# A small language-model layer on one core: gate and up weights under two scales, eight chunks split early, twelve of sixteen units of block 1 by fp16 halves

## The chip, the cores and the metric

The kernel runs on one NeuronCore of a Trainium2 chip. Its time is the device time of one execution in microseconds (us). The trace names the engines PE (TensorE matmuls), PEld (TensorE's loads of stationary operands), DVE (VectorE), ACT (ScalarE), POOL (GpSimd) and SP (SyncE, whose queue starts most DMAs).

## What is computed

The reference, with ids x of shape (2, 1024), vocabulary 128, width 512, 32 query heads and 8 key heads of width 16, hidden width 2048:

```python
h = rms_norm(rms_norm(emb[x]) * norm_w @ proj.T)          # token part
a = layernorm(h)
att = softmax(causal(q(a) @ k(a).T / 4)); h = h + (att @ v(a)) @ wo
g = layernorm(h)
h = h + (silu(g @ w_gate.T) * (g @ w_up.T)) @ w_down.T    # FFN
```

As there are only 128 different tokens, keys and values are tables over the vocabulary, and the weights of the attention are multiplied by counts of how often a token has been seen.

## The kernel before, in words

The 2048 tokens are eight **blocks** of 256, each of two tiles of 128. Block n's attention runs beside the FFN of block n-1, in `phase(n, att, ffn, m)`, which every engine goes through on its own in 24 **slots**; block 0 has no FFN beside it. Nothing is scheduled by a tool: which engine does what in which slot is written out in tables of slots (`FIRST_SLOTS`, `SECOND_SLOTS`, `HI_FIRST`, ...), each engine works through its own list in order, and semaphores hold it where it needs another engine. An engine that waits holds back all that stands behind it in its list.

**A unit of attention** V (16 a block, one a slot in slots 0 to 15) is one key head of one tile with its four query heads: PE transposes the queries into PSUM (`turn`, L1062), `stack` copies them to SBUF (ACT in blocks 0 and 1, L504; DVE later, L809), PE makes scores (`score`, L1073), ACT their exponentials (L529), DVE clips them and multiplies by the counts (L843), PE multiplies by the values (`values`). The last step has two forms. A `wide` unit takes the float32 weights as they are (L1091), two slots after its scores. A unit by **halves** is split into two fp16 parts, high by ACT (L539), low by POOL (L394), and takes eight short fp16 matmuls (L1097, L1098), three slots after its scores. All of block 0 is wide, all from block 2 on is halves; in block 1 `HALF_PAIRS` says which pairs of units are halves. `TAIL_PAIRS` says which pairs use another PSUM bank.

**A chunk of the FFN** j (16 a block) is gate and up for 128 hidden values: 24 matmuls on PE (L1120, L1121, L1125) in slot j, then in slot j+1 ACT's tanh (L521), two DVE steps (L831, L836), ACT's fp16 high half (L533) and POOL's low half (L390). In slots 16 to 23 PE does the down product in eight parts.

**The weights** of the FFN arrive as float32, 24 chunks of 128x1024 in 12 pairs (0 to 15 gate and up, 16 to 23 down). Each chunk is split once into two fp16 halves after a scaling by a power of two: `split_high` on ACT (L497) at the end of a slot, `split_low` on DVE (L786) in the same slot or the next. The scale of gate and up, `s_gu`, comes from a bound: PE forms Gram matrices of all 16 chunks (`gate_up_gram`, L1053, 128 matmuls spread over the start of block 0), DVE takes the diagonal in slot 12 (`gate_up_diag`, L752), PE sums it in slot 13 (L1143), and DVE makes the scale in slot 13 (`weight_scales`, L756 to L760). The first four chunks are split in slots 13 to 23 of block 0 (`HI_FIRST`, `LOW_FIRST`), the other twenty in slots 0 to 19 of block 1 (`HI_NEXT`). Wo is split in slots 1, 2, 5 and 10 of block 0 under its own scale (L487 on ACT, L747 on DVE).

**Ends of blocks.** After the last units of a tile come the transposes of y (L1156), its fp16 halves (ACT L564, DVE L869), the Wo product (L1167 to L1173), the residual (L877), the layer norm, its transposes (L1178) and their halves (L573, L892), in slots from 11 on. In slot 22 DVE's `place_max` (L794 to L801) puts the next block's row maxima in place, and PE's first `turn` of the next block, in slot 23, waits for it:

```python
if att and n > 0 and s == 23 and n + 1 < BLOCKS:
    turn((n + 1) * UPB)          # begins with pe.wait_ge(m_rdy, tl + 1)
```

## Time and profile before

| | |
|---|---|
| median of 3 runs | 717.11 us (717.09 to 717.43) |
| the profiled execution | 717.22 us, its span 715.5 us |
| mean granted TensorE clock | 0.986 of full speed |
| PE busy | 688.6 us (96%) |
| DVE, ACT, POOL busy | 410.2 (57%), 333.4 (47%), 313.4 (44%) |
| block 0's attention and tail | about 47 to 91 us of the span |
| block 1's slots 0 to 15 | 94.2 to 149.4 us |
| DMA | 40.37 MB, most of it before 76 us |

Shares of the whole span are means over stages with different limits; the change lies in the first quarter of the span, so the stretches 44 to 91 us and 94 to 176 us are what is to be read. In rows in order of time the columns are start, duration, engine, line, operation, tiles; "x8" joins eight neighbours, and square brackets give the idle time of the engine just before and who ended it. The next instruction of an engine often starts a little before the shown end of the one before it, so the cost of a row in a queue is the distance from its start to the next start. A row of a stretch gives its length, then the busy us (and instructions) of PE, PEld, DVE, ACT and POOL, then the granted clock, the DMA share and GB/s. A row of the waits gives the us in total, the number of waits and the longest.

### The profile page before, as it was taken

The numbers are of one execution on the slowest core, as the hardware profiler recorded it, in microseconds if no ns is written. First come the engines' busy times: TensorE is split into PE (matmuls) and PEld (weight loads), VectorE is DVE, ScalarE is ACT, GpSimd is POOL, SyncE is SP. The second block draws the span as 40 slices with busy tenths as digits, with TensorE's granted clock in tenths as the row PEclk, the third lists the DMA queues.
The fourth block names the chain that finished last, engine by engine and source line by source line (L and its number), as shares of the span: only waits on it lengthen the run. The fifth ranks groups of instructions, "written<-read, shape, count | busy, mean of one in ns | idle before, by whom it ended". The sixth has DMA issues, their size and how long they took to land.

```text
span 715.5 us, 16315 instructions
## 1 busy us (share of the span) xinstructions
PE 688.6 (96%) x6399; PEld 525.3 (73%) x6399; DVE 410.2 (57%) x1019; ACT 333.4 (47%) x676; POOL 313.4 (44%) x410
## 2 busy tenths in 40 slices
PE   8459999999999999999999999999999999999998
PEld 5359688965997479866996589856996599747873
DVE  7767789886655465545656365445655465543320
ACT  6426377861665146621664156522663166512320
POOL 5020315761565436751675336552665256511220
PEclk9859999999999999999999999999999999999999
DMA  8759500011000110012000300011000200000000
GB/s 316 288 206 404 191 18 1 3 47 61 17 2 2 60 63 1 2 47 77 2 1 2 106 17 2 1 61 62 2 2 16 93 16 2 1 16 16 2 1 29
DMA packets 10459, 40.37 MB, mean 56 GB/s; under 512 B 1808, under 2 KB 2576, under 8 KB 8592
## 3 DMA queue, kind: packets, MB, share of 16 engines
q1 hardware_dynamic: 6912, 25.44, 9.1%
q0 software_dynamic: 3328, 13.11, 5.9%
q8 instruction: 51, 0.84, 0.5%
q10 hardware_dynamic: 144, 0.79, 0.3%
q14 instruction: 24, 0.20, 0.1%
HBM read 29.89 MB, written 9.44 MB: 55 GB/s over the span
## 4 chain that ended last, share of the span: by engine, by line
PE 80%; DVE 10%; ACT 5%; issue 2%; DMA 1%; SPq 0%; ACTq 0%; DVEq 0%
PE banks L1120 13%; PE banks L1125 13%; PE banks L1121 13%; PE banks L1226 6%; PE banks L1228 6%; PE banks L1227 6%; PE banks L1073 3%; PE banks L1091 2%; PE banks L1167 2%; PE banks L1062 2%; PE banks L1173 2%; PE banks L1168 2%; DVE gate_work L831 2%; DVE ffn_weights L786 1%; PE banks L1053 1%
## 5 line engine op out<-in xcount | busy, mean ns | idle before, releaser
L1121 PE MATMUL banks<-xnT_and_h,ffn_weights 128*128 128x256 f16 x1024 | 237.3, 272 | 0.0
L1120 PE MATMUL banks<-xnT_and_h,ffn_weights 128*128 128x256 f16 x1024 | 237.2, 272 | 0.0
L390 POOL TENSOR_TENSOR gated_split<-gate_work,gated_split 128x256 f16<-128x256 f32 x128 | 88.4, 691 | 243.0 <-ACT gated_split L533 243.0
L1125 PE MATMUL banks<-xnT_and_h,ffn_weights 128*128 128x256 f16 x1024 | 153.6, 273 | 0.0
L394 POOL TENSOR_TENSOR weights_split<-weights,weights_split 128x512 f16<-128x512 f32 x104 | 123.2, 1185 | 0.0
L1120 PEld LDWEIGHTS banks<-xnT_and_h,ffn_weights 128*128 128x128 f16 x1024 | 100.4, 98 | 11.4
L1125 PEld LDWEIGHTS banks<-xnT_and_h,ffn_weights 128*128 128x128 f16 x1024 | 100.2, 98 | 11.6
L1121 PEld LDWEIGHTS banks<-xnT_and_h,ffn_weights 128*128 128x128 f16 x1024 | 99.9, 98 | 11.4
L521 ACT ACTIVATE gate_work<-banks,scales 128x256 f32<-128x256 f32 x128 | 60.6, 474 | 99.1 <-PE banks L1125 99.1
L529 ACT ACTIVATE weights<-banks,scales 128x512 f32<-128x512 f32 x128 | 87.3, 682 | 14.0 <-PE banks L1073 14.0
L843 DVE SCALAR_TENSOR_TENSOR weights<-weights,counts_T 128x512 f32<-128x512 f32 x128 | 87.6, 685 | 9.1 <-ACT weights L529 9.0
L809 DVE COPY q_stack<-banks 128x256 f16<-128x256 f16 x96 | 27.8, 290 | 103.0 <-PE banks L1062 103.0
L831 DVE SCALAR_TENSOR_TENSOR gate_work<-gate_work,banks 128x256 f32<-128x256 f32 x128 | 52.9, 413 | 58.7 <-ACT gate_work L521 58.2
L533 ACT ACTIVATE gated_split<-gate_work 128x256 f16<-128x256 f32 x128 | 53.3, 417 | 69.1 <-DVE gate_work L836 69.1
L1228 PE MATMUL banks<-ffn_weights,gated_split 128*128 128x512 f16 x224 | 84.9, 379 | 0.0
L1227 PE MATMUL banks<-ffn_weights,gated_split 128*128 128x512 f16 x224 | 84.9, 379 | 0.0
L1226 PE MATMUL banks<-ffn_weights,gated_split 128*128 128x512 f16 x224 | 84.8, 379 | 0.0
L539 ACT ACTIVATE weights_split<-weights 128x512 f16<-128x512 f32 x104 | 63.8, 613 | 0.0
L836 DVE SCALAR_TENSOR_TENSOR gate_work<-banks,gate_work 128x256 f32<-128x256 f32 x128 | 54.3, 425 | 4.4
L346 POOL DMA_INDIRECT token_rows<-token_table,indices x16 | 15.7, 980 | 89.1 <-DVE xnT_and_h L877 82.9
L573 ACT ACTIVATE xnT_and_h<-banks 128x512 f16<-128x512 f32 x16 | 9.6, 597 | 80.5 <-PE banks L1178 75.0
L1073 PE MATMUL banks<-q_stack,k_stack_even 128*128 128x128 f16 x256 | 42.7, 220 | 1.2 <-ACT q_stack L504 1.2
(236 smaller groups left out, 1043.4 us busy)
## 6 DMA issues: line engine op xcount, KB each, us to landing
ffn_weights<-in_ffn_w SPq DMA_DIRECT2D x12, 1024.0 KB, 9.9
out_rows_dram<-ffn_weights SPq DMA_DIRECT2D x16, 256.0 KB, 2.0
xnT_and_h<-in_wqkv SPq DMA_DIRECT2D x1, 1536.0 KB, 8.7
local_table<-gated_split SPq DMA_DIRECT2D x2, 640.0 KB, 5.3
local_table<-xnT_and_h SPq DMA_DIRECT2D x2, 640.0 KB, 5.8
gated_split<-in_projT SPq DMA_DIRECT2D x4, 256.0 KB, 4.3
ffn_weights<-in_wo SPq DMA_DIRECT2D x1, 1024.0 KB, 10.7
token_table<-weights_split ACTq DMA_DIRECT2D x1, 768.0 KB, 6.0
```

Source lines behind the costliest of these rows:

```text
L390: g.tensor_tensor(gtl[:, j, :], g2[j % 2], gth[:, j, :], ALU.subtract).then_inc(gt_lo, 1)
L394: g.tensor_tensor(WTl[V % RING], E[V % RING][:, :], WTh[V % RING], ALU.subtract).then_inc(wt_lo, 1)
L529: a.activation(E[V % RING][:, :], b_S[V % 2], ACT.Exp, scale=c_exp).then_inc(exp_done, 1)
L831: v.scalar_tensor_tensor(ag[j % 2], th[j % 2], 1.0, f_bank[j % 3][:, 0:BLK], ALU.add, ALU.mult).then_inc(a_rdy, 1)
L843: v.scalar_tensor_tensor(w, w, SEEN_MAX, cT[:, t * P:(t + 1) * P].unsqueeze(1).broadcast_to([P, REP, P]), ALU.min, ALU.mult).then_inc(w_rd ...
L1073: last = t.matmul(b_S[V % 2][:, (2 * j + a) * P:(2 * j + a + 1) * P], (KstA, KstB)[a][:, gr * P:(gr + 1) * P], Qst[:, r * 256 + j * P:r * ...
L1120: t.matmul(o, wh, xTh[m % 2][:, c, :], start=c == 0, stop=False)
L1121: t.matmul(o, wl, xTh[m % 2][:, c, :], start=False, stop=False)
L1125: last = t.matmul(o, gu_w(s, up, c, 0), xTl[m % 2][:, c, :], start=False, stop=c == DC - 1)
L1226: t.matmul(o, hh, dn_w(j, 0), start=j == 0, stop=False)
L1227: t.matmul(o, hh, dn_w(j, 1), start=False, stop=False)
L1228: last = t.matmul(o, hl, dn_w(j, 0), start=False, stop=j == HC - 1)
```

## The change

Gate and up get two scales. The first, for chunks 0 to 7, comes from sums of squares that ACT forms ahead of block 0 (`for i in range(EARLY // 2)`), summed over partitions by the same small matmul as Wo's; the second, for chunks 8 to 15, from Gram matrices of those chunks alone, now in slots 4 to 11. Where PE did the other Gram matmuls it now does narrow matmuls of no use to the output (`narrow_fill`). The eight early chunks are split from slot 3 of block 0 on, so that sixteen are left for block 1, on a new table of slots. Pairs 12 and 14 of block 1 join the halves (units 24, 25, 28 and 29 of the 16 to 31), pairs 11 and 13 leave the tail bank, and from unit 22 on DVE does the `stack` in place of ACT. `c_tanh` and the factor of L836 become columns per half. Line numbers of the changed kernel are 12 to 26 higher.

```diff
-HALF_PAIRS = (9, 11, 13, 15)
-TAIL_PAIRS = (9, 11, 13)
+HALF_PAIRS = (9, 11, 12, 13, 14, 15)
+TAIL_PAIRS = (9,)
+DVE_STACK = UPB + 6
+EARLY = 8
...
-HI_FIRST = {13: 0, 16: 1, 17: 2, 21: 3}
-LOW_FIRST = {13: (0,), 21: (1,), 22: (2,), 23: (3,)}
-HI_NEXT = {i - 4: i for i in range(4, NCH)}
+HI_FIRST = {3: 0, 6: 1, 8: 2, 10: 3, 13: 4, 17: 5, 21: 6, 22: 7}
+LOW_FIRST = {4: (0,), 7: (1,), 9: (2,), 11: (3,), 13: (4,), 21: (5,), 22: (6,), 23: (7,)}
+HI_NEXT = dict(zip((0, 1, 3, 5, 7, 8, 10, 11, 13, 14, 15, 16, 17, 18, 19, 20), range(EARLY, NCH)))
...
-GU_LEAD = (6, 12)
-GU_GRAM = {0: (12, 26), 1: (26, 38), **{s: (20 + 9 * s, 29 + 9 * s) for s in range(2, 12)}}
+LEAD_FILL = 10
+GU_FILL = {0: 16, 1: 14, 2: 10, 3: 9, **{s: 1 for s in range(4, 12)}}
+GU_GRAM = {s: (32 + 8 * s, 40 + 8 * s) for s in range(4, 12)}
...
-        s_q, s_k, s_v, s_wo, s_gu, s_d = (col(8 + i) for i in range(6))
-        r_q, r_k, r_v = (col(16 + i) for i in range(3))
-        c_exp, c_vo, c_tanh, c_gu, c_out, c_a = (col(20 + i) for i in range(6))
+        s_q, s_k, s_v, s_wo, s_d = (col(8 + i) for i in (0, 1, 2, 3, 6))
+        s_gu = [col(12), col(13)]
+        r_q, r_k, r_v, r_ga = (col(16 + i) for i in range(4))
+        c_exp, c_vo, c_gu, c_out, c_a = (col(20 + i) for i in (0, 1, 3, 4, 5))
+        c_tanh, c_pair = [[col(i), col(i + 1)] for i in (26, 28)]
...
-            sp.wait_ge(tab["wo_sq"], 1)
+            sp.wait_ge(tab["wo_sq"], 1 + EARLY // 2)
...
+            for i in range(EARLY // 2):
+                actq.wait_ge(ffn_in[i], 16)
+                if i > 0:
+                    actq.wait_ge(tab["wo_sq"], i)
+                a.activation(t_sq[:, (i + 1) % 2 * 2 * CH:((i + 1) % 2 + 1) * 2 * CH], raw_pair(i), ACT.Square, accum_out=pm[:, 36 + i:37 + i]).then_inc(tab["wo_sq"], 1)
...
-                    actq.wait_ge(tab["gu_scaled"], 1)
+                    actq.wait_ge(tab["scaled"], 1)
+                if i == EARLY:
+                    actq.wait_ge(tab["gu_scaled"], 2)
...
-                a.activation(half(i, 0), raw(i), ACT.Copy, scale=s_gu if i < 16 else s_d).then_inc(split_hi, 1)
+                a.activation(half(i, 0), raw(i), ACT.Copy, scale=s_gu[i // EARLY] if i < 16 else s_d).then_inc(split_hi, 1)
...
-                    if att and n <= 1 and s + 1 < UPB:
+                    if att and s + 1 < UPB and n * UPB + s + 1 < DVE_STACK:
...
-                root_powers(POWWO, f_bank[0][:, 0:1], 1)
-                v.tensor_scalar(s_wo, sc[:, 60:61], 2.0 ** 14, None, ALU.mult)
+                v.tensor_copy(pm[:, 44:45], f_bank[0][:, 0:1])
+                link(v.tensor_reduce(pm[:, 45:46], f_bank[0][:, 1:1 + EARLY // 2], AX.X, ALU.add))
+                root_powers(POWWO, pm[:, 44:46], 2)
+                v.tensor_scalar(sc[:, 11:13], sc[:, 60:62], 2.0 ** 14, None, ALU.mult)
+                v.tensor_scalar(r_ga, sc[:, 61:62], 1.0, None, ALU.mult)
                 v.tensor_scalar(c_vo, pw(POWV), pw(POWWO), 2.0 ** -14 / QKV_UP, ALU.mult, ALU.mult).then_inc(tab["scaled"], 1)
...
-                link(v.tensor_reduce(pm[:, 44:45], b_tail[:, P:2 * P], AX.X, ALU.max))
-                root_powers(POWG, pm[:, 44:45], 1)
-                v.tensor_scalar(s_gu, sc[:, 60:61], 2.0 ** 14, None, ALU.mult)
-                v.tensor_scalar(c_tanh, pw(POWG), 2.0 ** -26, None, ALU.mult)
-                v.tensor_scalar(c_gu, pw(POWG), pw(POWG), None, ALU.mult).then_inc(tab["gu_scaled"], 1)
-                dve.wait_ge(tab["gu_scaled"], 1)
+                link(v.tensor_reduce(pm[:, 46:47], b_tail[:, P:2 * P], AX.X, ALU.max))
+                root_powers(POWG + 1, pm[:, 46:47], 1)
+                v.tensor_scalar(s_gu[1], sc[:, 60:61], 2.0 ** 14, None, ALU.mult).then_inc(tab["gu_scaled"], 1)
+                v.tensor_scalar(sc[:, 26:28], sc[:, POWG:POWG + 2], 2.0 ** -26, None, ALU.mult)
+                v.tensor_tensor(sc[:, 30:31], pw(POWG), pw(POWG + 1), ALU.max)
+                link(v.tensor_tensor(sc[:, 31:32], r_ga, sc[:, 60:61], ALU.min))
+                v.tensor_scalar(c_gu, sc[:, 30:31], sc[:, 30:31], None, ALU.mult)
+                link(v.tensor_scalar(sc[:, 32:34], sc[:, POWG:POWG + 2], sc[:, 31:32], None, ALU.mult))
+                link(v.tensor_tensor(sc[:, 34:36], sc[:, 32:34], sc[:, 32:34], ALU.mult))
+                v.tensor_scalar(sc[:, 28:30], sc[:, 34:36], 2.0 ** -47, None, ALU.mult).then_inc(tab["gu_scaled"], 1)
+                dve.wait_ge(tab["gu_scaled"], 2)
...
-                    if att and n > 1 and s + 1 < UPB:
+                    if att and s + 1 < UPB and n * UPB + s + 1 >= DVE_STACK:
...
-                        v.scalar_tensor_tensor(g2[j % 2], f_bank[j % 3][:, BLK:2 * BLK], 2.0 ** -47, ag[j % 2],
+                        v.scalar_tensor_tensor(g2[j % 2], f_bank[j % 3][:, BLK:2 * BLK], c_pair[j // EARLY], ag[j % 2],
...
-            pe.wait_ge(tab["wo_sq"], 1)
-            t.matmul(f_bank[0][:, 0:1], ones32, pm[:, 35:36], start=True, stop=True).then_inc(tab["wo_sum"], 1)
+            pe.wait_ge(tab["wo_sq"], 1 + EARLY // 2)
+            t.matmul(f_bank[0][:, 0:1 + EARLY // 2], ones32, pm[:, 35:36 + EARLY // 2], start=True, stop=True).then_inc(tab["wo_sum"], 1)
...
-                    last = t.matmul(f_bank[2][:, 0:P], w, w, start=u == 0, stop=u == 127)
+                    last = t.matmul(f_bank[2][:, 0:P], w, w, start=u == 64, stop=u == 127)
                 return last
+
+            def narrow_fill(count):
+                for _ in range(count):
+                    t.matmul(b_tail[:, 0:P], id16[:, :], cT[:, 0:P], start=True, stop=True)
...
+                    if n == 0:
+                        narrow_fill(GU_FILL.get(s, 0))
...
-            gate_up_gram(0, GU_LEAD[0])
+            narrow_fill(LEAD_FILL)
             turn(0)
-            gate_up_gram(*GU_LEAD)
+            narrow_fill(LEAD_FILL)
```

What this does to an engine's list is seen in the order of its instructions. DVE, block 0, slots 8 to 12, before: L843 is the clipping of a unit, L850 and L853 end a pair of units, L747 is Wo's low half, L869 that of y, and the last row is the Gram diagonal.

```order
L843 SCALAR_TENSOR_TENSOR weights1<-weights1,counts_T 128x512
L747 SCALAR_TENSOR_TENSOR wo_split<-ffn_weights,scales,wo_split 128x1024
L843 SCALAR_TENSOR_TENSOR weights2<-weights2,counts_T 128x512
L850 RECIPROCAL rden1<-banks 128x8
L853 TENSOR_TENSOR xnT_and_h1<-banks,rden1 128x128
L869 TENSOR_TENSOR yT_split<-banks,yT_split 128x512
L843 SCALAR_TENSOR_TENSOR weights0<-weights0,counts_T 128x512
L752 TENSOR_TENSOR gate_work<-banks,ident 128x128
```

The same place in the changed kernel (L863, L870 and L873, L762, L889, and L767 for the diagonal):

```order
L870 RECIPROCAL rden0<-banks 128x8
L873 TENSOR_TENSOR y<-banks,rden0 128x128
L806 SCALAR_TENSOR_TENSOR ffn_weights<-ffn_weights,scales 128x1024
L863 SCALAR_TENSOR_TENSOR weights1<-weights1,counts_T 128x512
L762 SCALAR_TENSOR_TENSOR wo_split<-ffn_weights,scales,wo_split 128x1024
L863 SCALAR_TENSOR_TENSOR weights2<-weights2,counts_T 128x512
L870 RECIPROCAL rden1<-banks 128x8
L873 TENSOR_TENSOR xnT_and_h1<-banks,rden1 128x128
L889 TENSOR_TENSOR yT_split<-banks,yT_split 128x512
L806 SCALAR_TENSOR_TENSOR ffn_weights<-ffn_weights,scales 128x1024
L863 SCALAR_TENSOR_TENSOR weights0<-weights0,counts_T 128x512
L767 TENSOR_TENSOR gate_work<-banks,ident 128x128
```

Three of the new rows L806, the low halves of chunks 1 to 3, stand ahead of the diagonal; the one of chunk 0 stands further up, in slot 4.

DVE, end of block 1, slots 21 and 22, before: L888 is the normalised row block, and the three rows of `place_max` follow it.

```order
L888 TENSOR_SCALAR xn<-xnT_and_h1,ln_stats 128x512
L794 TENSOR_TENSOR max_local0<-max_local0,max_group0 128x32
L799 TENSOR_SCALAR token_rows0<-max_local0 128x2x16
L801 SCALAR_TENSOR_TENSOR token_rows0<-max_local0,token_rows0 128x2x16
L892 SCALAR_TENSOR_TENSOR xnT_and_h1<-banks,xnT_and_h1 128x4x128
```

In the changed kernel:

```order
L908 TENSOR_SCALAR xn<-xnT_and_h1,ln_stats 128x512
L806 SCALAR_TENSOR_TENSOR ffn_weights<-ffn_weights,scales 128x1024
L814 TENSOR_TENSOR max_local0<-max_local0,max_group0 128x32
L819 TENSOR_SCALAR token_rows0<-max_local0 128x2x16
L821 SCALAR_TENSOR_TENSOR token_rows0<-max_local0,token_rows0 128x2x16
L912 SCALAR_TENSOR_TENSOR xnT_and_h1<-banks,xnT_and_h1 128x4x128
```

The low half of the last chunk (L806), which stood a slot earlier, now lies between the normalised rows and `place_max`.

PE, from the small sum ahead of block 0 to slot 0, before (L1053 the Gram matmuls, L1062 a `turn`, L1073 scores):

```order
L1044 MATMUL banks<-part_max,xnT_and_h 128x1
L1053 MATMUL banks<-ffn_weights 128x128 x6
L1062 MATMUL banks<-ident,token_rows 128x128 x2
L1053 MATMUL banks<-ffn_weights 128x128 x6
L1073 MATMUL banks<-q_stack,k_stack_even 128x128
L1073 MATMUL banks<-q_stack,k_stack_odd 128x128
L1073 MATMUL banks<-q_stack,k_stack_even 128x128
L1073 MATMUL banks<-q_stack,k_stack_odd 128x128
L1062 MATMUL banks<-ident,token_rows 128x128 x2
L1053 MATMUL banks<-ffn_weights 128x128 x14
```

In the changed kernel (L1078 the narrow fill, L1086 the turn, L1097 scores):

```order
L1064 MATMUL banks<-part_max,xnT_and_h 128x5
L1078 MATMUL banks<-counts_T,ident 128x128 x10
L1086 MATMUL banks<-ident,token_rows 128x128 x2
L1078 MATMUL banks<-counts_T,ident 128x128 x10
L1097 MATMUL banks<-q_stack,k_stack_even 128x128
L1097 MATMUL banks<-q_stack,k_stack_odd 128x128
L1097 MATMUL banks<-q_stack,k_stack_even 128x128
L1097 MATMUL banks<-q_stack,k_stack_odd 128x128
L1086 MATMUL banks<-ident,token_rows 128x128 x2
L1078 MATMUL banks<-counts_T,ident 128x128 x16
```

Twelve Gram matmuls ahead of the first scores have become twenty fills, and fourteen behind them sixteen.

## Rows read from the trace of the kernel before

**Rows 1.** busy time by engine in two stretches, named in each row
```profile
56.00:78.00 22.00, 21.94 (x249) 19.76 (x246) 17.31 (x47) 13.13 (x25) 0.00 (x0) 1.00 0.94 375
...
94.00:152.00 58.00, 56.48 (x582) 50.17 (x583) 51.67 (x84) 48.26 (x96) 30.88 (x31) 1.00 0.01 2
```

**Rows 2.** PE up to slot 0 of block 0, and its clock
```profile
47.53 1.70 PE L1053 MATMUL banks<-ffn_weights 128*128 128x128 bf16 x14
...
50.00:52.00 2.00, 2.00 (x27) 2.00 (x26) 1.50 (x7) 1.80 (x3) 0.00 (x0) 0.88 0.80 319
```

**Rows 3.** ACT in order of time, slots 0 and 1 of block 0
```profile
46.48 0.38 ACT L504 ACTIVATE q_stack<-banks 128x256 f16<-128x256 f16 x1 [16.79 <-PE banks L1062]
...
51.07 1.15 ACT L487 ACTIVATE wo_split<-ffn_weights,scales 128x1024 f16<-128x1024 f32 x1 [0.20 <-DVE scales L742]
```

**Rows 4.** DVE in order of time, slots 4 to 13 of block 0
```profile
56.56 0.69 DVE L843 SCALAR_TENSOR_TENSOR weights<-weights,counts_T 128x512 f32<-128x512 f32 x1
...
59.24 1.28 DVE L747 SCALAR_TENSOR_TENSOR wo_split<-ffn_weights,scales,wo_split 128x1024 f16<-128x1024 f32 x1
60.43 1.41 DVE L843 SCALAR_TENSOR_TENSOR weights<-weights,counts_T 128x512 f32<-128x512 f32 x2
...
70.81 0.28 DVE L752 TENSOR_TENSOR gate_work<-banks,ident 128x128 f32<-128x128 f32 x1
...
75.40 1.28 DVE L786 SCALAR_TENSOR_TENSOR ffn_weights<-ffn_weights,scales 128x1024 f16<-128x1024 f32 x1 [1.35 <-ACT ffn_weights L497]
```

**Rows 5.** DVE: what it waited for between 56.5 and 70.85
```profile
DVE weights L843 <- ACT weights L529: 2.6, 4, 1.0
```

**Rows 6.** PE in order of time, slots 13 and 16 of block 0
```profile
71.14 0.49 PE L1143 MATMUL banks<-gate_work,xnT_and_h 128*128 128x128 f32 x2
...
77.43 0.81 PE L1091 MATMUL banks<-v_full_one,weights 128*128 128x17 f32 x6
```

**Rows 7.** PE in block 1: first matmul of slots 5 to 10 and 15
```profile
108.76 0.22 PE L1073 MATMUL banks<-q_stack,k_stack_even 128*128 128x128 f16 x1
...
112.34 0.23 PE L1073 MATMUL banks<-q_stack,k_stack_even 128*128 128x128 f16 x1 [0.26 <-ACT q_stack L504]
...
117.08 0.22 PE L1073 MATMUL banks<-q_stack,k_stack_even 128*128 128x128 f16 x1
...
120.90 0.22 PE L1073 MATMUL banks<-q_stack,k_stack_even 128*128 128x128 f16 x1
...
123.85 0.22 PE L1073 MATMUL banks<-q_stack,k_stack_even 128*128 128x128 f16 x1
...
127.01 0.22 PE L1073 MATMUL banks<-q_stack,k_stack_even 128*128 128x128 f16 x1
...
145.04 0.22 PE L1073 MATMUL banks<-q_stack,k_stack_even 128*128 128x128 f16 x1
```

**Rows 8.** ACT in order of time, slots 8 and 15 of block 1
```profile
122.29 0.47 ACT L521 ACTIVATE gate_work<-banks,scales 128x256 f32<-128x256 f32 x1
...
123.71 0.42 ACT L533 ACTIVATE gated_split<-gate_work 128x256 f16<-128x256 f32 x1 [0.37 <-DVE gate_work L836]
...
124.55 1.13 ACT L497 ACTIVATE ffn_weights<-ffn_weights,scales 128x1024 f16<-128x1024 f32 x1
...
148.08 0.59 ACT L564 ACTIVATE yT_split<-banks 128x512 f16<-128x512 f32 x1
```

**Rows 9.** PE, slot 16 of block 1: the first Wo matmul
```profile
149.44 0.39 PE L1167 MATMUL banks<-wo_split,yT_split 128*128 128x512 f16 x1
```

**Rows 10.** one line of the kernel on POOL: duration ns min/median/max
```profile
L394 POOL TENSOR_TENSOR weights_split<-weights,weights_split x104: 1151/1157/2144, 105.7 to 626.7; 128x512 f16<-128x512 f32 x104
```

**Rows 11.** DVE, slot 22 of block 1, and PE in slot 23
```profile
173.17 0.18 DVE L794 TENSOR_TENSOR max_local<-max_local,max_group 128x32 f32<-128x32 f32 x1
...
173.67 0.30 DVE L801 SCALAR_TENSOR_TENSOR token_rows<-max_local,token_rows 128x32 f16<-128x32 f32 x1
...
174.49 0.28 PE L1062 MATMUL banks<-ident,token_rows 128*128 128x128 f16 x2
```

4 lines of the change are left out of this document (2 added, 2 removed).

## The prediction

> **What bounds the kernel now.** I read the stretches first, then each engine in order of time. In block 0's attention PE is full, but DVE has work for 17.3 of 22.0 us [rows 1]; its gaps up to the Gram diagonal are four waits for ACT, 2.6 us together [rows 5]. In block 1 PE has 56.5 of 58.0 us, with DVE at 51.7 and ACT at 48.3 [rows 1], so three engines are near their limit and PE is the one that is full. A slot of block 1 is read from one first score matmul to the next [rows 7]: slot 8, in which no `values` stand, takes 123.85 - 120.90 = 2.95; slot 9, with one unit by halves, 127.01 - 123.85 = 3.16; slot 7, with one wide unit, 120.90 - 117.08 = 3.82. A wide unit thus costs PE 0.87, one by halves 0.21. From block 2 on nothing is changed but the source of one factor (L836), on an engine with slack there. The account is of the stretches 45 to 91 and 94 to 176 us.
>
> **Squares ahead of block 0: 0.** ACT forms four sums of squares of 128x2048. Its copy with scale of half that width takes 1.13 [rows 8], so I take 2.2 each, 8.8 together. ACT is idle 16.8 us ahead of its first `stack` [rows 3]; that hides them. Were that cover gone, PE's small sum would come up to 8.8 later.
>
> **Fills for Gram matmuls: +0.7.** Fourteen Gram matmuls occupy 1.70 from first start to last end, a pitch of 0.107 [rows 2]; the fills have the same 128 columns, so the same pitch. Eight more ahead of the first scores are 0.86, two more in slot 0 0.2, two more in slot 1 under 0.2. The clock is at the lower of its two levels (0.50, 1.2 GHz) and a mean of 0.88 over 50 to 52 puts its rise to 2.4 GHz at 50.5 [rows 2]. PE is no less busy before it with fills, so I let it rise at the same time; what is still to do then goes at double speed, which takes back some 0.4. But ACT's Wo half in slot 1 waits for DVE's scale, with 0.20 of idle time [rows 3], and that scale now comes behind a later first unit, with two more short steps. I take 0.7 for all that follows; at best the extra fills lie in slack, 0; at worst none of it is given back, 1.2.
>
> **Four splits into slots 3 to 12 of block 0: +2.0 more.** ACT has room: a split is 1.04 of its list (1.13 less the overlap) [rows 8], and only the first, behind the two Wo halves, makes the next `stack` late, by about 0.15. DVE has not. Before, unit 4 is clipped at 56.56 and the Gram diagonal starts at 70.81: 14.25, of which 2.6 idle, leaves 11.65 of work [rows 4, 5]. A low half of 128x1024 (Wo's is as wide) occupies 59.24 to 60.43, 1.2 [rows 4], and four of them now stand ahead of the diagonal: 4.8. The clip of unit 4 comes about 1.0 later, for the late start (0.7 + 0.15) and the order in which ACT does split and exponential. The list then has no gap: 56.56 + 1.0 + 11.65 + 4.8 = 74.0 for the diagonal, 3.2 later than 70.81. PE's sum of it stands in slot 13 ahead of Wo, the scores of unit 14 and all else, and follows 0.33 behind the diagonal (71.14) [rows 4, 6]; PE would be there by 72.8 and waits. Some comes back: before, DVE stood 1.35 for ACT's high half of chunk 0, which had waited for the scale, and so unit 14 was clipped late and PE's `values` of it began only at 77.43 [rows 4, 6]. Chunk 4 now has its scale long before. The longer scale in slot 13 eats about half of that. I give back 0.5: block 0's attention ends 3.2 - 0.5 = 2.7 later, 0.7 of it from above, 2.0 from here. The tail up to 91 us is one chain and moves as a whole. Bounds: 1.8 together (no late start, DVE then at the diagonal by 73) and 3.4.
>
> **Four wide units by halves in block 1: -2.6.** 4 x (0.87 - 0.21) = 2.64 on a full PE [rows 7].
>
> **Fewer splits and stacks in block 1: -1.1.** Slot 5 takes 3.58 against 3.16, and slot 6 4.74 against 2.95 + 0.87 + 0.21 = 4.03: 0.42 + 0.71 of waits [rows 7], the first on ACT's `stack` as the 0.26 of idle time at 112.34 says. With no split in slots 2, 4 and 6 and unit 22 stacked by DVE, I take both as gone.
>
> **ACT at the end of block 1: +1.0.** From tanh to the FFN's high half ACT needs 122.29 to 123.71, 1.42; that half and a unit's high half take 0.84 more; a split 1.04 [rows 8]. That is 3.3, in every other slot some 0.3 more for a copy of value sums (an estimate), where PE's slot is now 3.16. Slots 10 and 11, 13 and 14 have splits: ACT comes out of slot 12, which has none, some 0.35 behind, slot 13 adds 0.2 and slot 14 0.45, 1.0 in all. Before the Wo product stands a chain: ACT's copy of y started at 148.08, Wo 1.36 later [rows 8, 9]. In slot 15 the copy now starts 1.0 + 1.42 + 0.84 = 3.3 in, Wo at 4.6; PE is there at 3.5 (the 4.40 of before [rows 7, 9], less 0.66 for the unit and 0.25 for the wait already in it). It waits 1.1 instead of 0.25: 0.9, and 0.1 for a PSUM bank that ACT frees late in slot 12. Bounds 0 and 2.5.
>
> **The last low half ahead of `place_max`: +0.7.** The chain on DVE is tied to PE's Wo product, so 1.2 of low half moves `place_max` from 173.17 to 174.4; with its 0.80 (to 173.97) the maxima are ready at 175.2, where PE's `turn`, at 174.49 [rows 11], waits 0.7, and the last part of the down product behind it. Bounds 0.4 and 1.3.
>
> **Sum.** 0.7 + 2.0 - 2.6 - 1.1 + 1.0 + 0.7 = +0.7 on the profiled execution's 717.22 (span 715.5, 1.7 around it) gives 717.9; the median of the runs is 0.11 lower, so 717.8. A difference under 0.2%, 1.4 us, I call none.
>
> **Rivals.** *Faster: DVE's list in block 0 is absorbed.* It decides at the diagonal in slot 12: if DVE is there by 71 to 72, PE's sum never waits. For it: ACT and PE are ahead there and the idle time was DVE's alone. Against it: 4.8 of new work against 2.6 of gaps [rows 5]. With block 0 at +0.5 in place of +2.7 the time is 715.6 less the 0.6 that ACT's smaller backlog in block 1 would then also be worth: 715.0. Chance 0.23.
>
> *Slower: the late slots of block 1 are bound by ACT, DVE and POOL.* POOL's low half of a unit takes 1.15 at least and 2.14 at most [rows 10]. Its other work is at most (30.9 - 8 x 1.15) / 16 = 1.35 a slot [rows 1, 10], so a slot of POOL is 2.5 or 3.5 against PE's 3.16. If the long form holds in eight late slots, that is 0.33 in each, 2.6, of which I take 0.5 to be in the 1.0 already charged: 2.1 more, 719.9. It decides when POOL is more than 2 us behind, since the lag of three slots covers that much. Chance 0.22. The Trainium skill, page SBUF — State Buffer, section Who interferes with whom, has the rule: DVE and GpSimd share one port pair as an exclusive lock, and an instruction with two SBUF inputs on the one fully blocks a reading one on the other. By that rule each of the four added POOL steps may cost its 1.0 in full, 4.0 on POOL, and the sum would be up to 2 higher; the trace agrees with it, in its 2.14 beside 1.15.
>
> *The halves give PE nothing.* If the slots of block 1 were paced by ACT and not by PE, -2.6 falls away: 720.4. Against it, slot times differ exactly by what PE does. Chance 0.08.
>
> **Numbers.** The forecast, 717.8 with a range of its own from 716.6 to 719.0, has 0.47. Range 714.9 to 720.2: about half of the first and of the last rival lie outside. Faster 0.25 (the first rival and a little of the forecast), slower 0.35 (the other two and 0.05), same 0.40.
>
> **What the profile after would show.** Right: the low half of chunk 3 directly ahead of a diagonal near 74, PE idle in slot 13 until it; scores of unit 9 of block 1 and on 3.16 apart; PE idle ahead of the Wo product of block 1 and ahead of the `turn` in slot 23. Wrong: a gap on DVE ahead of the diagonal; a clock that rises earlier or later than 50.5; slots of block 1 over 3.4.

## The result and the profile after

The changed kernel took 722.07 us in the median of 4 runs (721.79 to 722.35), against 717.10 (716.70 to 717.43) for the kernel before on the same chip: a ratio of 1.0069, 95% interval 1.0053 to 1.0085. That is 5.0 us, or 0.7%, slower, outside the range of the prediction. The profiled execution took 721.79 with a span of 720.0; before, 717.22 and 715.5.

The first view to read is again the stretches of the whole core: from and to, then for each engine the busy time, then the granted clock, the DMA share and GB/s. The first two rows answer to [rows 1].

```profile
58.00:80.00 22.00, 20.21 (x214) 17.11 (x212) 20.59 (x49) 13.49 (x24) 0.00 (x0) 0.92 0.84 318
99.00:157.00 58.00, 55.75 (x590) 48.41 (x591) 49.70 (x91) 44.18 (x85) 36.48 (x38) 1.00 0.01 2
74.00:75.00 1.00, 0.00 (x0) 0.00 (x0) 1.00 (x4) 1.00 (x1) 0.00 (x0) 1.00 1.03 426
75.00:76.00 1.00, 0.99 (x5) 0.61 (x6) 0.97 (x4) 0.00 (x0) 0.00 (x0) 0.93 0.91 354
76.00:78.00 2.00, 2.00 (x6) 0.76 (x5) 1.72 (x13) 0.00 (x0) 0.00 (x0) 0.50 0.24 81
78.00:79.00 1.00, 1.00 (x3) 0.30 (x2) 0.93 (x3) 0.00 (x0) 0.00 (x0) 0.50 0.02 8
79.00:80.00 1.00, 1.00 (x10) 0.64 (x9) 0.64 (x1) 0.00 (x0) 0.00 (x0) 0.86 0.00 0
80.00:82.00 2.00, 2.00 (x22) 1.76 (x20) 0.69 (x1) 1.30 (x3) 0.00 (x0) 1.00 0.00 0
```

In block 0's stretch the slack of 4.7 on DVE has become 1.4 (20.59 of 22.00), and the mean granted clock is 0.92. From 74 to 75 PE does nothing. Behind it the clock goes from 1.00 to 0.93 and then to 0.50, the lower of its two levels (1.2 GHz instead of 2.4), and is back at 1.00 by 80. In block 1's stretch PE is busy 55.75 of 58.00 where it was busy 56.48, and POOL has 36.48 instead of 30.88.

PE in order of time, with the idle time before a row and what ended it in brackets. The rows are the scores of slot 4; the two waits of block 0 (64.26 and 75.00) with the Wo product behind the second; the first scores of block 1 (99.05); in block 1 the two waits for ACT's copy of the value sums (`pv`), the one at the Wo product and the one of the `turn` in slot 23; and the first scores of block 2 (181.29).

```profile
55.91 0.22 PE L1097 MATMUL banks<-q_stack,k_stack_even 128*128 128x128 f16 x1
...
64.26 0.59 PE L1115 MATMUL banks<-v_full_one,weights 128*128 128x17 f32 x4 [0.57 <-DVE weights L863]
...
75.00 0.49 PE L1167 MATMUL banks<-gate_work,xnT_and_h 128*128 128x128 f32 x2 [1.19 <-DVE gate_work L767]
...
75.33 0.38 PE L1191 MATMUL banks<-wo_split,yT_split 128*128 128x512 f16 x1
...
79.61 0.22 PE L1097 MATMUL banks<-q_stack,k_stack_even 128*128 128x128 f16 x1
...
99.05 0.23 PE L1097 MATMUL banks<-q_stack,k_stack_even 128*128 128x128 f16 x1 [0.47 <-ACT q_stack L516]
...
134.89 0.19 PE L1121 MATMUL banks<-v_hi_lo_one,weights_split 128*128 128x33 f16 x1 [0.30 <-ACT pv L567]
...
141.86 0.19 PE L1121 MATMUL banks<-v_hi_lo_one,weights_split 128*128 128x33 f16 x1 [0.48 <-ACT pv L567]
...
152.80 0.39 PE L1191 MATMUL banks<-wo_split,yT_split 128*128 128x512 f16 x1 [0.89 <-DVE yT_split L889]
...
178.58 0.29 PE L1086 MATMUL banks<-ident,token_rows 128*128 128x128 f16 x2 [0.57 <-DVE token_rows L821]
...
181.29 0.22 PE L1097 MATMUL banks<-q_stack,k_stack_even 128*128 128x128 f16 x1
```

The wait of 1.19 stands where the prediction put it. The wait of 0.57 in slot 8, ahead of the values of unit 6, was not in it, and neither was what follows the 1.19: the Wo product, from 75.33 to 79.61, took 4.28 us, against 74.06 - 71.47 = 2.59 for the same twelve matmuls in the kernel before, because nearly all of it lies in the stretch at 0.50. DVE's rows say why PE waited: the clip of unit 4 starts at 58.35, 1.79 later than before (forecast 1.0, and 0.73 of it is the late start shown in the table below), and behind it stand the added low halves, the last of them that of chunk 3 at 72.87, then a clip and the diagonal. From 58.35 to the diagonal are 16.32 us, where the prediction added up 11.65 + 4.8 = 16.45.

```profile
58.35 0.69 DVE L863 SCALAR_TENSOR_TENSOR weights<-weights,counts_T 128x512 f32<-128x512 f32 x1 [0.23 <-ACT weights L541]
...
72.87 1.27 DVE L806 SCALAR_TENSOR_TENSOR ffn_weights<-ffn_weights,scales 128x1024 f16<-128x1024 f32 x1
74.06 0.68 DVE L863 SCALAR_TENSOR_TENSOR weights<-weights,counts_T 128x512 f32<-128x512 f32 x1
74.67 0.28 DVE L767 TENSOR_TENSOR gate_work<-banks,ident 128x128 f32<-128x128 f32 x1
```

Last, DVE's gated product (the first row is of the kernel before, line 836 there; min, median and max ns). It is the one thing changed in blocks 2 to 7, and it got 59 ns longer.

```profile
L836 DVE SCALAR_TENSOR_TENSOR gate_work<-banks,gate_work x112: 424/425/426, 181.3 to 692.4; 128x256 f32<-128x256 f32 x112
```

```profile
L856 DVE SCALAR_TENSOR_TENSOR gate_work<-banks,scales,gate_work x112: 483/484/486, 185.4 to 697.0; 128x256 f32<-128x256 f32 x112
```

Cut at five marks that each trace has (ACT's first copy into the key tables, the scores of slot 4, the first scores of blocks 1 and 2, the end), the 4.5 us between the two spans lie as follows. The last two columns are experiments, told below.

| stretch, us | before | changed | fills_slot_8_and_13 | constant_and_fills |
|---|---|---|---|---|
| start to ACT's copy | 25.81 | 26.54 | 25.71 | 25.70 |
| to the scores of slot 4 | 28.63 | 29.37 | 29.37 | 29.36 |
| to block 1 | 39.78 | 43.14 | 41.81 | 41.83 |
| block 1 | 82.97 | 82.24 | 82.25 | 81.32 |
| blocks 2 to 7 and the end | 538.31 | 538.71 | 538.76 | 537.99 |
| span | 715.5 | 720.0 | 717.9 | 716.2 |

A difference of 0.4 in the third row need not come from the code: the last stretch of block 0, from slot 15 to the first scores of block 1, took 17.81 in this profile of the changed kernel and 18.19 in a second one (run 8), in which PE waited 0.19 at the second Wo product of block 0; in the kernel before it took 18.53.

### The profile page after: what moved, and what is told of

It is laid out like the page before. It is cut to its first block, busy times and chain, and to the rows that moved or that the text cites. A ratio compares the mean times of both kernels' runs of the same rounds, so it can differ in the third digit from the quotient of the medians.

```text
span 720.0 us, 16375 instructions
## 1 busy us (share of the span) xinstructions
PE 689.8 (96%) x6412; PEld 524.6 (73%) x6412; DVE 420.5 (58%) x1037; ACT 339.9 (47%) x678; POOL 317.5 (44%) x416
## 4 chain that ended last, share of the span: by engine, by line
PE 78%; DVE 13%; ACT 4%; issue 3%; POOL 1%; ACTq 0%; DVEq 0%; POOLq 0%
PE banks L1144 13%; PE banks L1145 13%; PE banks L1149 13%; PE banks L1254 6%; PE banks L1252 6%; PE banks L1253 6%; PE banks L1097 3%; DVE ffn_weights L806 2%; DVE weights L863 2%; PE banks L1191 2%; PE banks L1192 2%; PE banks L1197 2%; PE banks L1086 2%; DVE gate_work L851 2%; PE banks L1121 1%
## 5 line engine op out<-in xcount | busy, mean ns | idle before, releaser
L399 POOL TENSOR_TENSOR weights_split<-weights,weights_split 128x512 f16<-128x512 f32 x108 | 128.9, 1193 | 0.0
L863 DVE SCALAR_TENSOR_TENSOR weights<-weights,counts_T 128x512 f32<-128x512 f32 x128 | 88.7, 694 | 9.1 <-ACT weights L541 8.9
L829 DVE COPY q_stack<-banks 128x256 f16<-128x256 f16 x106 | 30.6, 289 | 100.0 <-PE banks L1086 100.0
L551 ACT ACTIVATE weights_split<-weights 128x512 f16<-128x512 f32 x108 | 66.3, 614 | 0.0
L856 DVE SCALAR_TENSOR_TENSOR gate_work<-banks,scales,gate_work 128x256 f32<-128x256 f32 x128 | 62.0, 484 | 4.6
L1097 PE MATMUL banks<-q_stack,k_stack_even 128*128 128x128 f16 x256 | 42.8, 221 | 0.9 <-ACT q_stack L516 0.9
```

The costliest lines, as they stand in the source:

```text
L399: g.tensor_tensor(WTl[V % RING], E[V % RING][:, :], WTh[V % RING], ALU.subtract).then_inc(wt_lo, 1)
L551: a.activation(WTh[V % RING], E[V % RING][:, :], ACT.Copy).then_inc(wt_hi, 1)
L863: v.scalar_tensor_tensor(w, w, SEEN_MAX, cT[:, t * P:(t + 1) * P].unsqueeze(1).broadcast_to([P, REP, P]), ALU.min, ALU.mult).then_inc(w_rd ...
```

## The experiments

Fifteen runs, in the order in which they were made. The mean granted clock of an execution turned out to be the main thing to read beside its time, so it is given where it differs. In rows of stretches that have one engine's busy time alone, that engine is PE.

**1. The diagonal ahead of the low half.**

```
-LOW_FIRST = {..., 9: (2,), 11: (3,), 13: (4,), ...}
+LOW_FIRST = {..., 9: (2,), 13: (3, 4), ...}
```

> The changed kernel, with the low half of chunk 3 moved from slot 11 to slot 13 of block 0, behind the Gram diagonal and the scale, so that nothing but its place on DVE's list differs. In the changed kernel PE waited 1.19 us for the diagonal, and its granted clock then stood at 0.50 for most of four us, in which the Wo product took 4.28 instead of 2.59. Theory wait-and-clock (the wait and the fall of the clock that follows it are two thirds of the loss): the diagonal comes 1.2 earlier, near 73.5, PE does not wait, the clock stays at 1.00 and the Wo product takes 2.6; 2.9 less in block 0, of which up to 0.6 is given back because unit 14 is clipped behind one more low half: 719.2 to 719.8. Rival list-only (DVE is short of time, and a wait removed at the diagonal comes back at unit 14 or at the Wo product): 721.5 to 722.1. Rival fills (the loss stems from the fills at the start of block 0 and from the late clock there): under 0.3 gained.

Measured: 722.84 to 729.12 in 6 executions, median 727.15, clock 0.971 to 0.981; ratio 1.0143 (1.0119 to 1.0167). PE no longer waited for the diagonal, and the Wo product took 2.59 again. But unit 14 was clipped behind two low halves, and PE waited there, with the same fall behind it:

```profile
80.52 0.59 PE L1115 MATMUL banks<-v_full_one,weights 128*128 128x17 f32 x4 [1.16 <-DVE weights L863]
```

```profile
80.00:81.00 1.00, 0.48 (x5) 1.00 0.00 0
...
82.00:84.00 2.00, 2.00 (x14) 0.50 0.01 3
84.00:86.00 2.00, 2.00 (x19) 0.50 0.96 280
86.00:88.00 2.00, 2.00 (x19) 0.53 0.33 127
88.00:90.00 2.00, 2.00 (x11) 1.00 0.00 0
```

So the list-only rival holds in its mechanism, though the loss is larger than the 721.5 to 722.1 that it gave: DVE is short of time, and a wait taken away at one place comes back at the next. And the fall follows PE's idle time wherever that is.

**2. Fills in the wait.**

```
                     if n == 0 and s == GU_SUM_SLOT:
+                        narrow_fill(20)
                         pe.wait_ge(tab["gu_diag"], 1)
```

> The changed kernel with 20 more narrow fill matmuls (128 columns, about 0.055 us each at the upper clock, 1.1 us together) on PE directly ahead of its wait for the Gram diagonal in slot 13 of block 0. DVE's list is untouched, so the diagonal and everything that needs it come when they came; only PE is busy instead of idle. Theory wait-and-clock: the granted clock stays at 1.00 behind the sum and the Wo product takes 2.6 instead of 4.28; 1.7 gained or a little less: 720.3 to 720.8. Rival: the fall of the clock at 76 has nothing to do with the idle 1.2 us before it (it comes from how busy PE was over a longer stretch, or from elsewhere): it stays at 0.50 there and the time is 721.9 to 722.4.

In the profiled execution (719.55, clock 0.986) the clock stayed up over the same product, as the windows show, and the stretch from slot 4 to block 1 took 41.44 instead of 43.14: the fall of the clock was worth 1.70.

```profile
74.00:75.00 1.00, 0.93 (x7) 1.00 0.92 382
75.00:76.00 1.00, 1.00 (x7) 1.00 0.39 126
76.00:78.00 2.00, 2.00 (x18) 1.00 0.00 0
```

But the other six executions took 725.4 to 731.75 with a clock of 0.970 to 0.976 (median of the seven 730.5, ratio 1.0202, 1.0189 to 1.0215), worse than any of the changed kernel so far. Something else let the clock fall, and for longer.

**3. As many fills as there were Gram matmuls.**

```
-LEAD_FILL = 10
-GU_FILL = {0: 16, 1: 14, 2: 10, 3: 9, ...
+LEAD_FILL = 6
+GU_FILL = {0: 14, 1: 12, 2: 9, 3: 9, ...
```

> The changed kernel with as many narrow fills as the kernel before had Gram matmuls there: 6 and 6 ahead of block 0 instead of 10 and 10, 14, 12, 9, 9 in slots 0 to 3 instead of 16, 14, 10, 9. In the changed kernel the first scores came 1.50 later (0.73 of it older than any changed instruction), the third 1.72 later, and the clock rose near 52.0 instead of 50.5. Theory fills-cost: 0.8 less ahead of the first scores, and with PE at the upper clock from the same time as before the change: 0.8 to 1.3 gained, 720.8 to 721.3. Rival fills-keep-the-clock (the clock needs PE busy without gaps, and the fewer fills leave PE waiting for ACT's stack and DVE's clip): first scores 0.8 earlier, but the clock rises at 52 or later and nothing is left by slot 4: 721.9 to 722.4. Rival DVE-decides (DVE's full list up to the diagonal takes up any start that is earlier only as far as DVE itself starts earlier): the diagonal moves by 0.4 to 0.8.

719.33 to 726.85, median 720.52, clock 0.972 to 0.986, ratio 1.0063 (1.0037 to 1.0089). In its profile the first scores came no earlier, for PE waited 0.92 at the first `turn` for the rows that DVE places. Inconclusive on the fills: this wait depends on a transfer (DVE had waited 1.37 for the DMA that brings the maxima), and the kernel before has it too in one profile of four (0.70, in run 5).

**4. Six pairs by halves in the kernel before, with one tail pair.**

```
-HALF_PAIRS = (9, 11, 13, 15)
-TAIL_PAIRS = (9, 11, 13)
+HALF_PAIRS = (9, 11, 12, 13, 14, 15)
+TAIL_PAIRS = (9,)
```

> The kernel before with one edit alone: pairs 12 and 14 of block 1 by fp16 halves too (six pairs of eight instead of four) and only pair 9 in the tail bank. One scale, splits and stacks as before. Theory halves-save-PE: each of four wide units saves PE 0.66, 2.6 at most; since no split is taken out of block 1 here, ACT and POOL bound some of these slots and 1.0 to 2.6 is left: 714.5 to 716.1 against 717.1. Rival ACT-bound (block 1 is paced by ACT, each unit by halves adds 0.84 to ACT's slot, and the splits are all still there): no gain or a loss, 717 to 719. Rival bank (one tail pair instead of three makes PE wait at pairs 11 to 13 for ACT to free the bank): waits of 0.5 or more named after ACT's copy of the value sums in slots 10 to 14, 0.5 to 1.5 of the gain lost.

718.54 in the median, ratio 1.0027 (1.0016 to 1.0038): slower by 2.0, where the prediction's term was -2.6. Block 1 took 84.89 instead of 82.97. PE waited three times for ACT's copy of the value sums:

```profile
131.67 0.19 PE L1097 MATMUL banks<-v_hi_lo_one,weights_split 128*128 128x33 f16 x1 [1.42 <-ACT pv L555]
...
139.06 0.19 PE L1097 MATMUL banks<-v_hi_lo_one,weights_split 128*128 128x33 f16 x1 [0.91 <-ACT pv L555]
...
146.45 0.19 PE L1097 MATMUL banks<-v_hi_lo_one,weights_split 128*128 128x33 f16 x1 [1.02 <-ACT pv L555]
```

```profile
136.00:148.00 12.00, 10.07 (x117) 8.92 (x116) 9.57 (x15) 10.90 (x23) 11.18 (x11) 1.00 0.01 2
```

In 136 to 148 ACT is busy 10.90 of 12, and what is left of it are its 0.37 waits for the gated product within each slot; two slots took 7.40, 3.70 each against PE's 3.16. POOL is busy 11.18 of the 12 and has no room either.

**5. The same with three tail pairs.**

```
-HALF_PAIRS = (9, 11, 13, 15)
+HALF_PAIRS = (9, 11, 12, 13, 14, 15)
```

> The kernel before with pairs 12 and 14 of block 1 by halves too, as in before_six_halves, but with the three tail pairs (9, 11, 13) kept. With one tail pair block 1 took 84.89 from its first scores to those of block 2 (82.97 before), PE waited 1.42, 0.91 and 1.02 for ACT's copy of the value sums, and ACT had no gap but its 0.37 waits for the gated product: two slots took 7.40. Theory ACT-list (six halves and a split in every slot are more than ACT can do in PE's time; the bank is only where PE notices): the waits move to ACT's other products (stack, yT_split), block 1 takes 84.0 to 84.9, time 1.0 to 2.0 above that of before. Rival bank (one tail pair too few is what costs): the three waits of 3.35 vanish, block 1 takes 81.5 to 82.3, time 0.7 to 1.5 below that of before.

719.83 in the median, ratio 1.0036 (1.0023 to 1.0049); block 1 took 84.89 again, to the hundredth. The bank's waits became others: for POOL's low halves, for ACT's copy ahead of the transposes of y, for the Wo product.

```profile
138.35 0.18 PE L1097 MATMUL banks<-v_hi_lo_one,weights_split 128*128 128x33 f16 x1 [0.59 <-POOL weights_split L394]
...
142.22 0.19 PE L1097 MATMUL banks<-v_hi_lo_one,weights_split 128*128 128x33 f16 x1 [0.55 <-POOL weights_split L394]
...
147.25 0.63 PE L1156 MATMUL banks<-ident,y 128*128 128x128 f32 x4 [1.15 <-ACT pv L555]
...
151.66 0.39 PE L1167 MATMUL banks<-wo_split,yT_split 128*128 128x512 f16 x1 [0.96 <-DVE yT_split L869]
```

The bank is only where PE notices that ACT, and POOL behind it, are late.

**6 and 7. The changed kernel with four pairs by halves, and with six pairs and three tail pairs.**

The first:

```
-HALF_PAIRS = (9, 11, 12, 13, 14, 15)
-TAIL_PAIRS = (9,)
+HALF_PAIRS = (9, 11, 13, 15)
+TAIL_PAIRS = (9, 11, 13)
```

The second:

```
-TAIL_PAIRS = (9,)
+TAIL_PAIRS = (9, 11, 13)
```

> The changed kernel with only the four pairs of the kernel before by halves (9, 11, 13, 15) and its three tail pairs; two scales, early splits and the rest as changed. Block 1 took 82.24 in the changed kernel and 82.97 before. Theory halves-save-PE (four wide units by halves save PE 2.64; what hides it in the changed kernel is 0.78 of waits for a bank and the 0.89 at the Wo product): 83.0 to 84.1. Theory ACT-list (the halves load ACT with 0.52 each, which PE gets back as waits, so that what block 1 gained came from fewer splits): 81.9 to 82.6, and no wait for ACT's copy of the value sums. In both the turn in slot 23 still waits 0.5 to 0.7 for the maxima.

> The changed kernel with three tail pairs (9, 11, 13) instead of one, six pairs by halves as changed. Theory bank: PE's waits of 0.30 and 0.48 for ACT's copy of the value sums go and block 1 takes 81.5 instead of 82.24. Theory ACT-list (ACT runs 0.9 behind PE at the end of block 1 whatever bank PE writes): PE gets 0.8 further ahead in slots 11 to 13 and then waits 1.6 to 1.7 instead of 0.89 at the Wo product; block 1 takes 82.1 to 82.3.

Block 1 took 82.57 with four pairs (82.24 with six), and 82.26 with six and three tail pairs, where the wait at the Wo product grew from 0.89 to 1.03 and waits of 0.56 for POOL and 0.31 for ACT's copy came in. The ACT-list theory holds in both by the length of block 1 (at the Wo product it had put 1.6 to 1.7 of wait): four units more by halves are worth 0.33, not 2.64. The times were 724.1 in both medians (ratios 1.0093 and 1.0104), and the profile of the first is of an execution at 0.972, which shows the long fall:

```profile
62.00:63.00 1.00, 1.00 (x17) 1.00 1.01 404
63.00:64.00 1.00, 0.43 (x8) 1.00 0.98 394
64.00:65.00 1.00, 1.00 (x12) 0.97 0.98 371
65.00:66.00 1.00, 1.00 (x13) 0.50 1.77 291
66.00:84.00 18.00, 18.00 (x109) 0.50 0.65 239
84.00:86.00 2.00, 2.00 (x8) 0.65 0.00 0
86.00:88.00 2.00, 2.00 (x23) 1.00 0.00 0
```

PE is idle for 0.57 at 63.9, ahead of the values of unit 6, for DVE's clip. The clock falls a microsecond later and stays at 0.50 for 20 us, through all the rest of block 0's attention; a slot takes 3.2 instead of 1.7. From slot 4 to block 1 are 50.22 us instead of 43.14. The wait of 0.57 is in the changed kernel too (64.26 above), with no fall behind it in that execution.

**8. The changed kernel again.**

> The changed kernel itself, once more, to see how its times spread. Three kernels that differ from it in one small step had executions with a mean granted clock of 0.970 to 0.976 and 6 to 11 us more, beside others at 0.981 to 0.986; the kernel before stayed at 0.986 in 14 of 14. Theory lottery (a wait of PE of about 1.2 us in slot 13 of block 0 is followed by a fall of the clock whose length varies from execution to execution; its four executions so far were at 0.981 to 0.983): times of 721.8 to 722.4 for most, and some of 725 to 730 with a clock under 0.977. Rival (the long falls belong to those kernels alone): all within 721.5 to 722.6 at 0.981 to 0.983. And of the 0.73 us by which all work from 8 us on was later in the changed kernel, before any instruction that differs: if it belongs to executions and not to the kernel, times cluster 0.6 to 0.7 apart in both kernels.

Three executions at 722.3 to 722.7 (clock 0.981 to 0.983) and three at 728.3 to 728.4 (0.972); the ratio to the kernel before, run beside it, was 1.0119 (1.0087 to 1.0151). The long falls are its own. ACT's first copy started at 26.68 here, and between 25.70 and 26.54 in all other profiles of either kernel's code, so the 0.73 at the start belongs to the execution. Block 0's two waits were there again, 0.56 and 1.19, and the same short fall behind the second, 0.50 from 76.6 to 79.7.

**9. Two scales alone.** The changed kernel with `HI_FIRST`, `LOW_FIRST`, `HI_NEXT`, `HALF_PAIRS`, `TAIL_PAIRS` and the stacks of block 1 as before:

```
-HI_FIRST = {3: 0, 6: 1, 8: 2, 10: 3, 13: 4, 17: 5, 21: 6, 22: 7}
+HI_FIRST = {13: 0, 16: 1, 17: 2, 21: 3}
...
-DVE_STACK = UPB + 6
+DVE_STACK = 2 * UPB
```

> The changed kernel without its early splits and without its new halves: two scales, squares by ACT, narrow fills and the factor from a column as changed, but chunks 0 to 3 split where the kernel before splits them (high halves in slots 13, 16, 17, 21 of block 0), chunks 4 to 23 in slots 0 to 19 of block 1, four pairs by halves, three tail pairs, all stacks of block 1 on ACT. Theory waits-make-falls (the early splits make PE wait 0.57 ahead of unit 8's values and 1.19 ahead of the Gram sum, and each such wait can be followed by a long fall of the clock): PE has no wait over 0.5 up to slot 16, the clock stays at 0.985 to 0.988 in all or all but one execution, and the time is that of before plus 0.74 (fills) plus 0.4 to 0.5 (0.12 in each of the blocks 2 to 7): 1.1 to 1.5 more than before. Rival fills-make-falls (Gram matmuls replaced by narrow fills are what unsettles the clock): executions at 0.970 to 0.983 here too, 3 to 11 us more than before.

(This text and the next name unit 8 for the first wait; it is unit 6, in slot 8.) 719.39 in the median, ratio 1.0031 (1.0019 to 1.0043), four executions at 0.985 or 0.986 and two at 0.983, none above 720.4. No execution has a long fall here, without the early splits. The 2.0 are more than the 1.1 to 1.5 expected, since block 1 took 83.87 instead of 82.97, with nothing changed in it but scale operands.

**10. Fills in two places, one of them wrong.**

```
+                if V == 8:
+                    narrow_fill(10)
```

> The changed kernel with narrow fills in both of PE's waits in block 0: 10 ahead of unit 8's values (wait of 0.57) and 20 ahead of the Gram sum (wait of 1.19). With the second alone, 1 of 7 executions kept 0.986 and the rest had 0.970 to 0.976. Theory waits-make-falls: most or all executions at 0.985 to 0.986 and 719.3 to 720.3, the spread of 6 to 11 us gone. Rival (the falls come from something else in this kernel, such as how much PE does in all of block 0 or when the DMA loads fall): the mix of 0.970, 0.976 and 0.986 stays, median over 724.

The wait of 0.57 stayed, since it stands ahead of unit 6, and so did the mix: clock 0.976 to 0.986, median 722.51, ratio 1.0078. The edit missed its place, which makes it a control for run 13: the same thirty fills, ten of them where PE does not wait, do not keep the clock up.

**11. Splits spread over block 1, the last low half behind the maxima.**

```
-... (0, 1, 3, 5, 7, 8, 10, 11, 13, 14, 15, 16, ...)
+... (0, 1, 2, 3, 4, 5, 7, 8, 9, 11, 13, 16, ...)
...
```

The second part of the edit, not shown, makes DVE do the last low half in slot 22, behind `place_max`.

> The changed kernel with its splits of block 1 in slots 0 to 5, 7, 8, 9, 11, 13 and 16 to 20 (so none in slots 10, 12, 14, 15, where the changed kernel has them in 10, 11, 13, 14, 15), and with the low half of the last chunk behind the placing of the maxima in slot 22. Block 1 took 82.24 in the changed kernel, of which PE waited 0.78 for ACT's copy of the value sums (1.1 by the slot lengths), 0.89 at the Wo product and 0.57 at the turn in slot 23. Theory ACT-list (ACT has 3.6 to 3.7 of work in a slot with a split and a half unit, 2.6 without a split, against PE's 3.16; the splits next to one another are what puts it behind): the waits for value sums and for Wo fall to under 0.3 together and the turn's goes, block 1 takes 80.0 to 80.8. Rival POOL-and-DVE (POOL's low halves of 1.2 to 2.1 beside DVE bound the late slots): a wait of 0.5 or more for POOL's weights_split, block 1 81.3 to 82.2. Time not read from the whole, which the clock disturbs, but from block 1.

From slot 8 to slot 14 each slot took 2.96 to 3.23, and the waits for the value sums and for Wo were gone, as the ACT-list theory wants. What was won there was lost in slots 5 and 6 (4.02 and 6.21 instead of 3.15 and 4.26): PE waited for DVE's stack, the clock fell behind that wait too (0.50 from 118 to 121), and at the end PE waited 0.47 for the low half in place of 0.57 for the maxima. Block 1 took 83.04, so neither theory's figure came; the median of the six was 723.78, ratio 1.0114. In its profile PE waited 0.57 and 1.18 in block 0 as in the changed kernel, and no fall came behind either.

```profile
115.48 0.23 PE L1097 MATMUL banks<-q_stack,k_stack_even 128*128 128x128 f16 x1 [0.70 <-DVE q_stack L829]
...
177.37 0.38 PE L1238 MATMUL banks<-ffn_weights,gated_split 128*128 128x512 f16 x1 [0.47 <-DVE ffn_weights L806]
```

**12. Stacks by DVE in the kernel before.**

```
-                    if att and n <= 1 and s + 1 < UPB:
+                    if att and n * UPB + s + 1 < UPB + 6 and s + 1 < UPB:
...
-                    if att and n > 1 and s + 1 < UPB:
+                    if att and n * UPB + s + 1 >= UPB + 6 and s + 1 < UPB:
```

> The kernel before with one edit alone: stacks of units 22 to 31 of block 1 by DVE instead of ACT. It takes 0.26 (0.42 by the slot lengths) of wait out of slot 5 and 0.27 a slot off ACT's list. Theory: block 1 82.4 to 82.6 instead of 82.97, time 0.4 to 0.6 below before. Rival (DVE, at 51.7 of 58 us there, gets late with its gated product, on which ACT and POOL wait, and slots 6 and later lengthen): 82.9 to 83.5.

Block 1 took 82.88; ratio 0.9999 (0.9990 to 1.0009). The wait of 0.26 for ACT became one of 0.46 for DVE. The theory's 82.4 to 82.6 did not come; 82.88 is at the low end of what the rival gave, and there is no gain.

**13. Fills where the two waits are.**

```
+                if V == 6:
+                    narrow_fill(10)
...
+                        narrow_fill(20)
                         pe.wait_ge(tab["gu_diag"], 1)
```

> The changed kernel with narrow fills in both of PE's waits of block 0, now where they are: 10 ahead of the values of unit 6 in slot 8 (wait of 0.57; the earlier run had them at unit 8 in slot 10, where PE does not wait) and 20 ahead of the Gram sum in slot 13. Theory waits-make-falls: at least five of six executions at 0.985 to 0.986 and 719.0 to 720.3, as no wait over 0.2 is left up to slot 16 but the one for ACT's first stacks. Rival (the falls come from elsewhere): as before a mix with 0.970 to 0.981 in half of them, median over 721.5.

All 5 executions had a clock of 0.986 or 0.988. The median was 720.26 (719.63 to 721.93), ratio 1.0052 (1.0040 to 1.0065).

```profile
62.00:66.00 4.00, 4.00 (x56) 1.00 1.02 349
66.00:72.00 6.00, 6.00 (x82) 1.00 1.00 395
72.00:74.00 2.00, 2.00 (x31) 1.00 1.04 422
74.00:76.00 2.00, 1.94 (x12) 1.00 0.95 392
76.00:80.00 4.00, 4.00 (x35) 1.00 0.17 58
```

**14 and 15. A constant factor, and both.**

```
-f_bank[j % 3][:, BLK:2 * BLK], c_pair[j // EARLY], ag[j % 2],
+f_bank[j % 3][:, BLK:2 * BLK], 2.0 ** -47, ag[j % 2],
```

> The changed kernel with the constant 2^-47 as factor of DVE's gated product instead of a value from a column (the kernel before has this constant; the scales' ratio is left out of the product, so this part of the computation is changed). In the trace the product takes 484 ns with the column and 425 with the constant. Theory column-costs (ACT waits for that product in every FFN slot, and PE for ACT at the value sums): blocks 2 to 7 take 78.67 each instead of 78.80, and block 1, where ACT is 0.9 behind at its end, 81.6 to 82.0 instead of 82.24; 1.0 to 1.4 in all where the clock is the same. Rival: DVE has slack, only the wait's name changes: 78.80 and 82.24 stay.

> The changed kernel with both: the constant factor (the scales' ratio left out, as in constant_factor) and narrow fills in PE's waits in slots 8 and 13 of block 0. If the falls of the clock come from these waits and the column costs 0.12 a block: clock at 0.985 to 0.986 in nearly all, time 717.8 to 718.6, so 0.6 to 1.4 above before, which is what fills (0.7), early splits (1.6) and block 1 (1.0 to 1.4 gained) leave. If either does not hold: 719 or more.

Both leave out the ratio of the two scales, so their output is not the layer's; they price the instruction and are no versions of the kernel.

The product took 424 ns again, blocks 2 to 6 took 78.66 to 78.68 instead of 78.79 to 78.80 each, and block 1 81.32 instead of 82.24, in the profiles of both. With the constant alone the median was 724.84 (ratio 1.0085), as the falls of the clock stay.

```profile
L856 DVE SCALAR_TENSOR_TENSOR gate_work<-banks,gate_work x111: 423/424/426, 190.9 to 699.2; 128x256 f32<-128x256 f32 x111
```

With constant and fills, 718.29 in the median of 11 (9 of them at 0.985 or 0.986, one at 0.963), ratio 1.0015 (1.0004 to 1.0025). No run beat the kernel before.

## Why the prediction was wrong

Forecast was +0.7 on the span; it came to +4.5 in the profiled execution. By its own steps:

- **Squares ahead of block 0, 0: right.** ACT did the four at 1.90 each, not 2.2, and still stood idle 9.6 before its first stack.
- **Fills, +0.7: right.** From ACT's first copy to slot 4 it is 29.37 - 28.63 = 0.74. All profiles with the ten and ten fills have 29.36 to 29.44; the four of the kernel before's code have 28.44 to 29.02, so the difference is known to some 0.4. "I let it rise at the same time" was not: the clock rose near 52.0 here and between 49.8 and 50.3 in the profiles of runs 1 to 3. A rise at another time than 50.5 was one of the prediction's own signs of being wrong, but it is not a property of the kernel, and the sum by slot 4 did not depend on it.
- **Four splits, +2.0: right in mechanism and size, wrong in what follows.** The diagonal came at 74.67 (forecast 74.0), and PE waited 1.19 for it. With the clock kept up by fills, slot 4 to block 1 took 1.66 more than before in run 2 and 2.03 to 2.05 more in runs 13 and 15. That this meets 2.0 is in part luck: from slot 4 to slot 15 it is 2.4 more, and the tail, which was to move as a whole, is 0.35 to 0.7 shorter than in the kernel before. PE's wait of 0.57 in slot 8 was not foreseen at all. The step that failed is the one not made: a wait of PE was costed at its own length. In the profiled execution the fall of the clock behind the 1.19 cost 1.70 more, and where a fall came behind the 0.57 in slot 8 and lasted, 8.4 (50.22 against 41.81 with fills in both waits).
- **Four wide units by halves, -2.6, with ACT at +1.0: wrong by their sum.** Going from four to six pairs was worth 0.33 in the changed kernel and cost 1.92 in the kernel before. PE's rows gave the right price for a unit, but PE was not alone at its limit in the late slots. The wait at Wo was sized well (0.89, forecast 0.9); "0.1 for a PSUM bank" was in truth 0.30 and 0.48 named and 1.1 by the slot lengths (3.63 and 3.81 for 3.16), slots over 3.4 being another of its signs of being wrong. Runs 5 and 7 show that this is ACT's lateness and not the bank: with the other bank the waits only move. With the constant these two slots took 3.22 and 3.69, so 0.53 of the 1.1 is the price of the column; no run has four pairs together with the constant, and what the halves alone would then be worth stays open.
- **Fewer splits, -1.1: nearly right.** Slot 5 took 3.15, as forecast; slot 6 took 4.26 and not 4.03, and 4.05 with the constant.
- **Last low half, +0.7: right**, 0.57.
- **"From block 2 on nothing is changed but the source of one factor, on an engine with slack there", 0: wrong, and worth 1.7.** DVE has slack, but each slot's chain runs tanh, product, ACT's copy, POOL, and ACT stood waiting for this product in every slot, 0.37 in block 1 and 0.39 from block 2 on; the 59 ns are added to that (0.46) and show at PE, once a block, as 0.40 instead of 0.27 ahead of the value sums. That is 0.12 to 0.13 in each block from 2 on, 0.8 in all, and 0.92 in block 1, where ACT has no slack. The trace had the row: the wait of 0.37 on ACT stands in [rows 8].

The sum closes. Without falls and without the column (constant_and_fills) the span is 716.2, 0.7 above before, which is the forecast (0.3 of it by luck: one later block of the kernel before took 78.93 instead of 78.67, in three of the four profiles of its code and in none of the changed code); the column adds 1.7 (716.2 to 717.9), the fall of the clock 1.7, the late start 0.8 (26.54 against 25.71), and the shorter last stretch of block 0 takes off 0.4, in which executions of the same code differ: 720.0, as measured. So the forecast's own errors (block 1 predicted 2.0 shorter, 1.65 shorter with the constant; slot 4 to block 1 +2.0, measured +2.05 in run 15) were small, and two mechanisms that it held to be nothing made the loss.

Of the rivals, the one on the late slots of block 1 was right that ACT and POOL bound them and gave 719.9, but most of its price came through the product's 59 ns, which it did not name. The rule it cited, of the port pair that DVE and GpSimd share, is borne out by the traces. Of POOL's 104 halves in the kernel before and 108 in the changed one, all seven of 2.14 us start while a low half of a chunk is under way on DVE, and none of the others does. The other way round, the low half on DVE took 1.28 in block 0, where POOL does nothing, and 1.76 where a step of POOL started with it:

```profile
114.44 1.76 DVE L806 SCALAR_TENSOR_TENSOR ffn_weights<-ffn_weights,scales 128x1024 f16<-128x1024 f32 x1
...
115.08 2.14 POOL L399 TENSOR_TENSOR weights_split<-weights,weights_split 128x512 f16<-128x512 f32 x1
```

(L399 is L394 of the kernel before; in POOL's part the lines are 5 higher, not 12 to 26.) So the long form does not hold in eight late slots, as the rival took it, but in those in which a low half of DVE runs. PE waited 0.51 for a POOL half in block 1 of the kernel before and 0.56 in run 7, but never in the changed kernel.

**That PE's waits bring the falls** rests on counts over all executions whose clock was read. Of the nine kernels in which PE waits 0.57 in slot 8 (the changed kernel's own two measurements taken together), 7 of 60 executions had a mean clock of 0.985 or more. Of the seven without that wait, the kernel before among them, 95 of 105 had. Fills in slot 13 alone did not help (1 of 7), nor did they with ten more at a place where PE doesn't wait (2 of 6); in both waits they did (5 of 5, and 9 of 11 with the constant). A wait is not all that it takes, though. No profile shows a fall behind the waits of 0.89 and 0.57 in block 1, nor behind those of 1.42, 0.91 and 1.02 in run 4, whose seven executions had 0.985 or 0.986; in block 1 only run 11 has one. And an execution of the kernel before had 0.965 and 732.56 us, without any of the waits added here. The Trainium skill, page TensorE: Matmul & The Clock Gate, section HAM oscillation — how this bites in real kernels, describes PE falling back to its lower clock behind waits for data, and tells it of waits for DMA of several microseconds. This case agrees in kind and not in size: its falls come behind waits of 0.57 to 1.19 us, and the measurement decides.

**What stays open:** why a fall ends after 4 us in one execution and after 13 or 20 in another, or does not come at all behind the same wait; why waits in block 0 bring falls and waits as long in block 1 hardly do; why 2 of the 5 executions in run 13 took some 1.5 us more at the same clock or a higher one; and how much of ACT's lateness in block 1 would go with a better order of the splits, since run 11 moved the trouble to slots 5 and 6.

## What to carry to other kernels

A wait on a TensorE that was full until then can cost more than its length: look for the idle stretches that the change makes (here 0.57 and 1.19 us in block 0), and price the fall of the clock behind them, in the worse executions too; if the wait can't be avoided, try dummy matmuls in it, which cost nothing here, and put them into every such wait. An instruction on an engine with slack still costs if another engine waits for that very instruction in each iteration: read the idle time ahead of its consumer, not the busy share of its engine. And when a step moves work from a full engine to two others, add up one iteration of each of them before taking the gain.

## What was not expected of the hardware

DVE's product of 128x256 from PSUM took 484 ns with its factor from a column in SBUF and 424 to 425 with a constant, in all instructions of either form. A wait of 0.57 us in block 0 was followed by 20 us at the lower clock in one execution and by none in another, and a wait of 1.42 us in block 1 by none. A POOL half of 1.15 us took 2.14 whenever a low half of DVE was already under way. The same code reached the same instruction, ACT's first copy into the key tables, anywhere from 25.70 to 26.68 us.
